# Attention maxima handed over in four turns in the first and last group of heads, and four output buffers

## The reference

```python
x = x + attention(layernorm(x))        # B=4, T=2048, C=256, 16 heads of 16
x = x + mixture(layernorm(x))          # 8 experts, the best 2 for each row
# attention, for each batch and head:
q, k, v = ...                          # low-rank projections, rotary on half of q and k
scores = einsum('bhqd,bhkd->bhqk', q, k) / sqrt(16)
scores = where(causal, scores, -inf)
att = softmax(scores, axis=-1)
y = einsum('bhqk,bhkd->bhqd', att, v)
```

## Time and profile before

| | us |
|---|---|
| median of 3 runs | 2733.09 |
| lowest, highest | 2732.42, 2741.71 |
| span of the profiled execution, first to last instruction | 2735.5 |
| attention in it | about 250 to 1942 |
| first maxima piece on PE | 258.2 |
| first exponential on ACT | 321.1 |
| last turn of maxima | 1814.6 |
| DVE busy / PE busy / ACT busy, whole span | 75% / 88% / 58% |

### The profile page before, as it was taken

How to read it: one execution, slowest core, us unless ns; L and a number is a source line. 1 busy time by engine, 2 the same in 40 slices (tenths; PEclk the granted TensorE clock), 3 DMA queues, 4 the chain that set the end, 5 groups by cost and what they waited for, 6 DMA issues and landing times. The chain is left out here.

```text
span 2735.5 us, 48214 instructions
## 1 busy us (share of the span) xinstructions
PE 2406.9 (88%) x15842; PEld 1359.7 (50%) x15842; DVE 2048.1 (75%) x5002; ACT 1581.1 (58%) x2716; POOL 823.7 (30%) x1130
## 2 busy tenths in 40 slices
PE   6885799999999999999999999998777389998998
PEld 6774333333334333333334333332444278887897
DVE  3876989998999898888898998940355457765776
ACT  3663277777777776667777777776433234433443
POOL 1543011211212112111212112121055655555554
PEclk8997699999999999989999999997888689999999
DMA  3777814414504513504414423010675323323332
GB/s 145 261 260 212 113 39 63 74 42 61 86 29 64 86 34 59 84 27 65 83 35 64 80 44 71 8 31 20 236 203 177 94 92 113 107 93 96 111 109 72
DMA packets 147501, 255.95 MB, mean 94 GB/s; under 512 B 72951, under 2 KB 91897, under 8 KB 138916
## 3 DMA queue, kind: packets, MB, share of 16 engines
q1 hardware_dynamic: 114544, 164.96, 27.1%
q0 software_dynamic: 29904, 80.65, 8.9%
q10 hardware_dynamic: 2812, 7.26, 1.5%
HBM read 147.59 MB, written 107.76 MB: 93 GB/s over the span
## 5 line engine op out<-in xcount | busy, mean ns | idle before, releaser
L836 ACT ACTIVATE prob<-ps_s 128x512 f32<-128x512 f32 (+5 forms) x1620 | 1078.1, 714 | 480.5 <-PE ps_s L932 477.8
L857 DVE TENSOR_REDUCE maxes<-ps_m 128x2 f32<-128x1024 f32 x768 | 913.9, 1221 | 107.8 <-PE ps_m L973 104.8
L932 PE MATMUL ps_s<-q_st,k_st 50*128 50x512 f32 (+3 forms) x2560 | 610.2, 413 | 73.8 <-ACT prob L836 57.2
L973 PE MATMUL ps_m<-k_st,q_st 48*128 48x512 f32 (+3 forms) x2560 | 603.2, 443 | 75.9 <-DVE maxes L857 39.6
L953 PE MATMUL ps_o<-prob,v_sb 128*17 128x512 f32 (+3 forms) x5120 | 617.5, 556 | 1.2 <-ACT prob L836 0.7
L802 POOL TENSOR_SCALAR_AFFINE_SELECT prob<-prob 128x256 f32<-128x256 f32 x512 | 203.2, 406 | 1347.8 <-ACT prob L836 1220.8
L973 PEld LDWEIGHTS ps_m<-k_st,q_st 48*128 48x128 f32 x2560 | 272.6, 191 | 531.3 <-DVE maxes L857 256.6
L861 DVE CUSTOM_DVE_ANT_0 junk<-ps_m,causal 128x128 f32<-128x128 f32 (+3 forms) x1024 | 453.1, 484 | 44.2 <-PE ps_m L973 42.7
L932 PEld LDWEIGHTS ps_s<-q_st,k_st 50*128 50x128 f32 x2560 | 318.3, 190 | 306.1 <-ACT prob L836 234.1
L1728 ACT ACTIVATE h_hi<-ps_turned 128x512 fp32r<-128x512 f32 x142 | 85.0, 598 | 225.6 <-PE ps_turned L1843 157.9
L94 PE MATMUL ps_out<-experts_hi,h_lo 128*128 (+1 forms) x568 | 173.0, 305 | 0.0
(11 more groups left out here) (187 smaller groups left out, 3180.6 us busy)
## 6 DMA issues: line engine op xcount, KB each, us to landing
parts_dram<-parts SPq DMA_DIRECT2D x64, 512.0 KB, 3.8
q_st<-parts_dram SPq DMA_DIRECT2D x84, 256.0 KB, 8.5
k_st<-parts_dram SPq DMA_DIRECT2D x84, 256.0 KB, 18.4
v_dram<-v_out SPq DMA_DIRECT2D x16, 544.0 KB, 5.5
xin<-in_L_attn_x SPq DMA_DIRECT2D x16, 512.0 KB, 6.0
ffn_raw<-in_L_ffn_W POOLq DMA_DIRECT2D x32, 256.0 KB, 5.2
y_dram<-y_sb SPq DMA_DIRECT2D x64, 128.0 KB, 2.0
split_hi<-ffn_hi POOLq DMA_DIRECT2D x16, 512.0 KB, 3.2
```

The costliest lines, as they stand in the source:

```text
L836: last_exp = nc.scalar.activation(prob[:, at:at + n, lo:TB], bank[:, 0:n, lo:TB], ACT.Exp, scale=DH ** -0.5)
L857: return nc.vector.tensor_reduce(maxes[:, 2 * pair:2 * pair + 2, qt, kc], bank[:, :, :], AX.X, ALU.max)
L932: mm = nc.tensor.matmul(ps_s[k % 2][:, i, lo:TB], k_st[half(h % 2, ROWS), w % BUFS, h // 2, kt * P:(kt + 1) * P], q_st[half(h % 2, ROWS), ...
L973: mm = nc.tensor.matmul(ps_m[slot][:, i, 0:wide], q_st[half(i, STACK), w % BUFS, pair, qt * P:(qt + 1) * P], k_st[half(i, STACK), w % BUFS ...
```

## The change

The first group hands over its maxima in four turns, one for each chunk, and the last group in four as well, but its chunks come in the order 3, 2, 1, 0, for the maxima and the scores alike. The other 14 groups keep their two turns. `y_sb` and `rec` get four buffers in place of two, and `maxes` two in place of one. The plan's rules and costs are unchanged, but it runs over the new lists. `BUFS`, `load` and the place where group 2 is loaded (right behind turn 0) are as they were.

```diff
-EARLY = 12
+YOUT = 4
+ALONE = [[c] for c in range(CH)]
+PARTS_OF = [ALONE if w == 0 else ALONE[::-1] if w == NG - 1 else [[0, 1, 2], [3]] for w in range(NG)]
+ORDER = [[c for part in parts for c in part] for parts in PARTS_OF]
+TURNS = [(w, i) for w in range(NG) for i in range(len(PARTS_OF[w]))]
-STEP_LIST = [(w, c, kt) for w in range(NG) for c in range(CH)
+STEP_LIST = [(w, c, kt) for w in range(NG) for c in ORDER[w]
...
-        y_sb = sb("y_sb", [P, 2, TILES, GH, DH], F32)
+        y_sb = sb("y_sb", [P, YOUT, TILES, GH, DH], F32)
...
-        maxes = sb("maxes", [P, GH, QT, CH], F32)
+        maxes = sb("maxes", [P, 2, GH, QT, CH], F32)
...
                 if e[0] == "turn_max":
                     sp.wait_ge(piece_taken, ring + 1)
-                    place_minus(e[1], e[2])
-                    if turn_number(e[1], e[2]) == 0:
+                    place_minus(e[1])
+                    if e[1] == 0:
                         for g in range(2, BUFS):
                             load(sp, g)
...
-                if c == CH - 1 and r == TILES - 1:
+                if c == ORDER[w][-1] and r == TILES - 1:
                     split_weights(w)
```

More of the change, by code:

```diff
@@ L498, in max_list @@
 def max_list():
-    turns = [(w, late) for w in range(NG) for late in (False, True)]
     out = []
-    for i, (w, late) in enumerate(turns):
-        tiles = range(EARLY, QT) if late else range(EARLY)
+    for j, (w, i) in enumerate(TURNS):
+        tiles = range(TURN_LO[j], TURN_LO[j] + TURN_TILES[j])
         pieces = [("max", w, qt, pair, kc) for qt in tiles for pair in range(2) for kc in range(qt // TILES + 1)]
-        turn = [("turn_max",) + turns[i - 1]] if i else []
-        out += pieces[:AHEAD] + turn + pieces[AHEAD:] + [("chain", w, late)]
-    return out + [("turn_max",) + turns[-1]]
+        turn = [("turn_max", j - 1)] if j else []
+        out += pieces[:AHEAD] + turn + pieces[AHEAD:] + [("chain", j)]
+    return out + [("turn_max", len(TURNS) - 1)]
 def attention_plan(groups, covers):
@@ L542, in attention_plan @@
             w, c, _ = STEP_LIST[newest]
-            placed = rows.get((w, c == CH - 1))
+            placed = rows.get(TURN_OF[w, c])
             if newest < s + DEEP and placed is not None:
@@ L574, in attention_plan @@
                 vector = max(start + 260, vector - 85) + 543
-                rows[e[1:]] = vector + 6500
+                rows[e[1]] = vector + 6500
             else:
@@ L675, in attend @@
         out_copied = sem("out_copied")
-        y_stored = [sem(f"y_stored{i}") for i in range(2)]
+        y_stored = [sem(f"y_stored{i}") for i in range(YOUT)]
         rec_made = sem("rec_made")
@@ L698, in plan_with_ring @@
                 ring += e[0] in ("max", "turn_max", "turn_out")
-        def turn_number(w, late):
-            return 2 * w + (1 if late else 0)
         def load_heads(eng, g, t, lo, hi, done):
@@ L723, in _, with place_minus @@
         def _(sp):
-            def place_minus(w, late):
-                lo, n = (EARLY, QT - EARLY) if late else (0, EARLY)
-                sp.dma_start(minus_dram[late][:, :, :, :].rearrange("s h k n -> (h k) s n"),
+            def place_minus(j):
+                w, lo, n = TURNS[j][0], TURN_LO[j], TURN_TILES[j]
+                sp.dma_start(minus_dram[n][:, :, :, :].rearrange("s h k n -> (h k) s n"),
                              minus_rows[0:GH * n, :, :].bitcast(F32)).then_inc(rows_out, 16)
-                sp.wait_ge(rows_out, 16 * (turn_number(w, late) + 1))
-                from_v = minus_dram[late].rearrange("s (pr par) k n -> s pr par (k n)", par=2)
+                sp.wait_ge(rows_out, 16 * (j + 1))
+                from_v = minus_dram[n].rearrange("s (pr par) k n -> s pr par (k n)", par=2)
                 for par in range(2):
@@ L757, in _ @@
                     load(sp, (e[1] + 1) // NSTEP + BUFS - 1)
-            for i in range(2):
-                sp.wait_ge(y_stored[i], 16 * (NG * CH // 2))
+            for u in range(YOUT):
+                sp.wait_ge(y_stored[u], 16 * (NG * CH // YOUT))
         @block.gpsimd
@@ L871, in _ @@
                 elif e[0] == "chain":
[L873 removed]
+                    lo, n = TURN_LO[e[1]], TURN_TILES[e[1]]
                     m = minus[:, 0:GH * n].rearrange("p (h n) -> p h n", h=GH)
                     dve.wait_ge(piece_taken, ring)
[L876 removed]
+                    nc.vector.tensor_reduce(m, maxes[:, TURNS[e[1]][0] % 2, :, lo:lo + n, :], AX.X, ALU.max,
                                             negate=True).then_inc(minus_made, 1)
                 elif e[0] == "turn_max":
[L879 to L880 removed]
+                    j = e[1]
+                    n = GH * TURN_TILES[j]
                     bank = ps_m[slot]
@@ L977, in _ @@
                     elif e[0] == "turn_max":
-                        n = GH * (QT - EARLY if e[2] else EARLY)
-                        pe.wait_ge(minus_made, turn_number(e[1], e[2]) + 1)
+                        n = GH * TURN_TILES[e[1]]
+                        pe.wait_ge(minus_made, e[1] + 1)
                         mm = nc.tensor.transpose(ps_m[slot][0:n, 0, 0:P], minus[:, 0:n], ident[:, :])
@@ L1894, in transformer_block @@
     v_dram = nc.dram_tensor("v_dram", (HG, P, B * T // P, GH, VW), F32).ap()
-    minus_dram = [nc.dram_tensor(f"minus_dram{late}", (PARTS, GH, n, P), F32).ap()
-                  for late, n in enumerate((EARLY, QT - EARLY))]
+    minus_dram = {n: nc.dram_tensor(f"minus_dram{n}", (PARTS, GH, n, P), F32).ap() for n in sorted(set(TURN_TILES))}
     y_dram = nc.dram_tensor("y_dram", (B * T, C), F32).ap()
```

55 lines of the change are left out of this document (29 added, 26 removed).

## The result

| | before | changed |
|---|---|---|
| median, us | 2732.76 (4 runs) | 2784.34 (4 runs) |
| lowest, highest | 2720.63, 2741.71 | 2774.91, 2810.24 |
| ratio (95% interval) | | 1.020 (1.013 to 1.027) |
| profiled execution: time; span | span 2735.5 | 2777.12; 2775.4 |

The change costs about 2%. The forecast was 2769 us, with a range that ended at 2784, so the time lies at its upper end, 0.3 us outside. The profiled execution is 39.9 us longer than that of before, where the sum had +36. Several of the terms that make it up are off by more than that, in both directions.

A forecast was written before the change was run, and what follows sets the result against it. DVE's list of maxima was taken to set attention's pace. Restart +42, turns +2, tail -8, buffers -4 and split +4 made +36, span 2771.5, so 2769 us as median; range for 8 in 10: 2746 to 2784.

The forecast's parts named there:

- the restart: First group, 35th maxima piece after PE's wait for turn 1's rows: starts at about 342.3 us, 47.6 us late.
- 56 us to group 0's last turn, as before: From the 35th piece to group 0's last turn: 56 us, unchanged, for the same pieces and two turns.
- 95 us for the 80 pieces behind it: Group 0's last turn to group 1's second: 95 us, was 100.4, with 119 products for 154; bounds 91 and 100.
- first stand: PE's wait at chunk 0's first product, for turn 0's rows behind group 0's load: about 9 us.
- The head start: Earlier score products in group 0: if nothing waits, 12 more done at the last turn, saving 8.2 us.
- The signs: Evidence to look for: SP queue times, PE and DVE waits, first exponential, turn times, tail, POOL's split and output buffer waits.
- The short stall: Rival: turn 1's rows arrive before about 307 us, leaving only the 9 us wait; sum -2, 2731 us; chance 0.07.
- The loss of 16: Rival: the product list bounds the walk and the long stall is there; +16, 2749 us; chance 0.10.
- The score list sets the pace: Rival: rows in time and the first product 32 us earlier moves everything; 2705 us; chance 0.03 for faster.
- Turns of group 15 and buffers together: Two more turns in group 15, +2; DVE's output buffer wait and the half clock behind it removed, -4.
- Tail: Score products left after the last maxima: 12 fewer at 0.68 us each, -8.
- Split: Splitting the last weights behind the final masks delays the next stage: +4, bounds 2 and 5.

The follow-up runs named there:

- e1: The changed kernel with load 2 issued behind turn 3 in place of turn 0: 2764.97 us, ratio 1.0139 to the kernel before.
- e5: The changed kernel with load 1 behind turn 1 and load 2 behind turn 3, both on SP's queue, and the last split early: 2686.63 us, ratio 1.0059.
- e9: As e5, with turn 0's rows due 10 us later in the plan, so more maxima precede the first product: 2737.51 us, ratio 1.0005.
- e12: e9's first group, with group 15 in two turns, chunk 3 first, then 2, 1, 0: 2743.36 us, ratio 1.0022.
- e15: The changed kernel with group 0 in three turns, SP's loads behind the first and last of them, and the split early: 2670.08 us, ratio 1.0001.
- e10: The kernel before with one 128x64 memset more on DVE for each maxima piece: 2732.97 us, ratio 1.0009.
- e13: The kernel before with one matmul of 128 columns more on PE for each maxima piece: 2752.74 us, ratio 1.0319.
- e14: As e9, with group 1 in three turns (chunk 0, chunks 1 and 2, chunk 3): 2700.02 us, ratio 1.014.
- e4: The changed kernel with all 16 groups at two turns and the old chunk order, leaving only the buffers changed: 2735.85 us, ratio 1.0025.
- e8: The changed kernel with group 0 back at two turns, group 15 in four turns, chunks 3 to 0, and the split early: 2673.15 us, ratio 1.0009.
- e2: The changed kernel with the last weights' split behind chunk 3's masks in group 15 too: 2794.94 us, ratio 1.0198.
- e16: The changed kernel run again with nothing changed, beside the kernel before on one chip: 2739.12 us, ratio 1.027.

## Why the forecast was right, and where it was wrong

**The step that failed** is the pace behind the restart: "56 us to group 0's last turn, as before" and "95 us for the 80 pieces behind it". Measured on PE's turns they are 62.7 (342.7 to 405.4) and 100.6 us (405.4 to 505.9), 12 us more, and the second turn came at 506 where 493 was forecast: +55 in place of +42. (The turn that the forecast put at 350.5 us before is at 351.3; by it the two were 56.7 and 99.5.)

The reason given was that the maxima on DVE set the pace. So the first way was taken as unchanged, since it has the same pieces, and the second as cheaper, since it has 119 products for 154. But the first way now holds 81 products, where it held 53, and it took 6 us more than before. And the second did not get cheaper: it took 100.6 us for 99.5, and 100 to 101 in e1, e5, e9, e12 and e15 as well, which have the same 119 products. e10 and e13 speak against DVE as the bound: DVE can take 35 us more for 2, while all that PE got was paid, with the reserves named there. The forecast's own rows had PE busier (93%) than DVE (89%).

Counted on PE there was nothing to make up. From the 34th piece to group 1's second turn there stood 128 pieces and 207 products before; now 128 pieces and 200 (215 less the 15 of chunk 0 that were done). That is nearly the same work, 156.2 us before and 163.2 now. The 7 us more go with the clock, 0.82 for 0.86. It isn't the stands that bring them: e9, without a stand, needs 160.3 us for this way at 0.84, and e1, e5 and e12 need 162 to 163 at 0.83 or 0.84, all with ACT's stop of 15.1 us. That the stops bring the half clock is what the rows show side by side (a stop of 15 us, then 0.50 and 0.67); no run takes the stops out alone. The forecast had the restart at half clock in its upper bound only, with 10 us.

**Right, and shown by an experiment.** Turn 1's write is held behind load 2 (31.7 us), two loads at once end together, the rows are there for PE at 341.2 us (forecast 341.5), the 35th piece is 48.0 us late (47.6). e1 takes this hold away and gives back 27.0 us at group 1's second turn, the 27.1 of the stand, and 19 at the same clock. e5 cuts the first stand to 9.3 us, e9 takes it away, and with the split early 2 us of the 42 are left. e14 makes the hold anew elsewhere.

**The head start is worth nothing**, even without a stand, where the forecast had 8 us for it (a tail shorter by 12 products): e9 and e15 have the first product 27 to 35 us earlier and are no faster. By the turns of e9 the lead is gone at group 1's second turn: it comes at 457.8 us, 6.9 later than before.

**The signs.** Of those that the forecast named, the order on SP's queue, turn 1's reads (338.5) and the gap ahead of chunk 1's product came. Turn 1's write was issued at 306.8 and not by 300, the first exponential came at 293.0 and not at 288, DVE stood 27.3 us and not 30, and the last turn, the tail and the border are the sizes below. PE as the bound was to show in more than 10 us made up behind the restart. It went with 7 us lost there; that sign was the wrong one for it.

**The other rivals.** The short stall falls with the 31.7 us of the hold. The rule named with it is 2 us and the bytes at 436 GB/s. The Trainium skill (DMA: Bandwidth & Descriptors, Anatomy of one DMA — SWDGE (gpsimd) path) gives it for a single DMA issued by GpSimd, and the forecast's 10.5 us, an estimate, used it for a load of 13 on another path. The rows have 28 to 30 us for such a load, and 22 to 24 to land its last piece alone, 50 beside another. The loss of 16, which counted the products alone, falls with the 55 us at the last turn. "The score list sets the pace", which had 32 us for an earlier first product, falls with e9 and e15, though PE is the bound: the plan is one list on PE, and products that are drawn forward push as many maxima back.

**Sizes that were off.** First stand: 9 forecast, 17.0 measured (reads beside a load land after 11 us, not 3); it changed nothing at the end of the second stand, which the DMA sets. Turns of group 15 and buffers together: -2, measured +0.2 over the walk; e4 gives the buffers 1 us or so, e8 the turns nothing that shows. Tail: -8, measured -26.5. Its count was right (12 products, and 13 matmuls in the rows), 8 us at 0.68 each; the rest is 0.57 us for each of the others in place of 0.68, by the clock. Twelve profiled executions in the new order have 0.57 to 0.62, six in the old order 0.58 to 0.72, so the order may help the clock there, but does not decide it, and what does stays open. Split: +4, measured +8.8. It was POOL's drain at the end of the stage that was missing: 5.3 us in both kernels, started at 1909.4 and hidden before. Now it can start only at 1974.0, behind the landing of the split, with nothing beside it. With the split early (e2) it starts right behind the last mask and costs 0.2 us.

**Luck.** The terms of the profiled execution (measured less forecast: +13 at the restart, +2 for turns and buffers, +5 at the split, +2 behind, -18 in the tail) nearly cancel, so that +36 stood against +39.9. That is luck, and mostly the clock of one tail. The medians, over more executions, are +51.6 and, in e16, +65.8 us apart. The difference to the +42 at the same clock is the lower clock that goes with the change: in e16's runs 0.0137, at 20.2 us for each 0.01 = 28 us. The profile shows where it comes from. Up to 510 us there are about 64 us more at half clock than before (0.71 for 0.83 from 250 us on), 64 x 0.5 / 2775 = 0.012. Of these 48 lie ahead of the restart, in the head and the stands, where the clock is 0.50 in both kernels but the time is 48 us longer, and 16 behind it. So most of the lower clock is the lost time itself, counted by the clock, and not a second price behind it. Whether the walk behind a stand also gets a lower clock stays open: the three profiled executions with the second stand have 0.98, 0.96 and 0.95 in it, e1, e5, e9, e12 and e15 without it 0.96 to 0.98.

## What to carry to other kernels

A small transfer that something waits for must not stand behind a bulk load in its queue: before turns are made finer, list what each queue holds ahead of them, and count whether a product needs the rows before the load has landed. Where one engine takes two lists in one fixed order, an earlier start of one list pushes back the other, and a stand in it delays both; ask what that engine has left after the stand. Before a term is taken "as before", count what both lists have in that stretch, and not the list alone that is thought to set the pace. What is last in a stage shows costs that were there before, hidden.

## What the hardware showed that I had not expected

- A drain of 5.3 to 5.6 us on POOL at the end of a stage in which it had issued DMAs, in all 18 profiles. It was free in the kernel before, where POOL was done 27 us ahead of the last exponential, cost 0.2 us in e2, where it started right behind the last mask, and was exposed whole in the changed kernel, where it waited for the landing of the split.
- Two small reads of rows take 3 us to land on an idle set of DMA engines, and 11 us beside a load of 3.7 MB on another queue.
- The clock, not the work, makes most of the scatter between executions: 20 us for 0.01 of mean granted clock, and a last turn 40 us apart in two executions of one and the same kernel. Differences of 0.1% could be read only after that was taken out.
